# Grouped convolution in 32-row TensorE tiles on unshuffled x, with staggered tiles, in a fused convolution and mixing kernel

## What is computed

```python
# x: (64, 128, 2048) f32; c = cond_128: (64, 128); weight: (128, 32, 9); 4 groups
y = x + conv1d(x, weight, padding=4, groups=4) + (c @ c_weight.T)[:, :, None] + bias[None, :, None]

h = gelu(c @ W0 + b0); h = gelu(h @ W1 + b1)
att = softmax(h @ W2 + b2)                     # (64, 8)
agg_w = einsum('bk,koi->boi', att, weight_k)   # one 128x128 matrix per sample
agg_b = att @ bias_k
out = y + einsum('boi,bih->boh', agg_w, y) + agg_b[:, :, None]
```

## Time and profile before

| | us |
|---|---|
| profiled execution, device time | 839.29 |
| its span, first to last instruction | 837.4 |
| mean granted clock of TensorE | 0.977 of full |
| TensorE matmul busy | 766.2 (92%) |
| TensorE weight load busy | 600.9 (72%) |
| ScalarE busy | 637.2 (76%) |
| GpSimd busy | 552.1 (66%) |
| VectorE busy | 410.1 (49%) |
| DMA share of 16 engines, whole span | 91.5% |
| moved by DMA | 242.9 MB |

### The profile page before, as it was taken

How to read it: one execution, slowest core, us unless ns; L and a number is a source line. 1 busy time by engine, 2 the same in 40 slices (tenths; PEclk the granted TensorE clock), 3 DMA queues, 4 the chain that set the end, 5 groups by cost and what they waited for, 6 DMA issues and landing times.

```text
span 837.4 us, 15303 instructions
## 1 busy us (share of the span) xinstructions
PE 766.2 (92%) x5424; PEld 600.9 (72%) x5424; DVE 410.1 (49%) x299; ACT 637.2 (76%) x291; POOL 552.1 (66%) x596
## 2 busy tenths in 40 slices
PE   2659998999999999999999999999999999999994
PEld 2547776777777777777777777777777777777773
DVE  6662455445445555444555445445554444554430
ACT  7766886888778877878786787888777868866554
POOL 3289686667778767767876666668667566866620
PEclk9988999999999999999999999999999999999997
DMA  5778999999999999999999999999999999987643
GB/s 194 206 230 263 309 317 292 305 326 306 325 314 330 313 313 308 318 301 306 329 318 306 297 312 312 319 331 332 305 314 300 284 305 327 319 257 247 220 164 126
DMA packets 91011, 242.90 MB, mean 290 GB/s; under 512 B 15914, under 2 KB 58482, under 8 KB 74610
## 3 DMA queue, kind: packets, MB, share of 16 engines
q1 hardware_dynamic: 90994, 242.67, 91.5%
HBM read 101.57 MB, written 75.50 MB: 211 GB/s over the span
## 4 chain that ended last, share of the span: by engine, by line
SPq 46%; PE 20%; DMA 20%; ACT 6%; issue 6%; POOL 1%; DVE 0%; POOLq 0%
SPq L240 34%; DMA mix_dram<-mix_parts 16%; PE ps L366 12%; SPq L264 9%; PE ps L383 8%; DMA mix_rep<-mix_dram 3%; ACT z_out L448 3%; SPq L272 2%; ACT x_ph L429 1%; ACT x_cv L452 1%; DMA x_in<-in_x_dram 1%; ACT z_out L452 0%; SPq L214 0%; PE ps L353 0%; POOL mix_prod L646 0%
## 5 line engine op out<-in xcount | busy, mean ns | idle before, releaser
L448 ACT ACTIVATE z_out<-ps,par 128x2048 f32<-128x2048 f32 x64 | 253.3, 3957 | 143.0 <-PE ps L383 143.0
L515 DVE TENSOR_TENSOR y_lo<-ps,y_hi 128x1024 fp32r<-128x1024 f32 x128 | 156.4, 1222 | 305.9 <-ACT y_hi L438 305.9
L429 ACT ACTIVATE x_ph<-x_in 128x2048 f32<-128x2048 f32 x63 | 246.5, 3914 | 0.0
L366 PE MATMUL ps<-x_hi,cw_hi 128*128 128x512 f32 x768 | 228.6, 406 | 0.3 <-DVE y_lo L515 0.3
L366 PE MATMUL ps<-x_hi,cw_lo 128*128 128x512 f32 x768 | 221.3, 397 | 0.0
L366 PE MATMUL ps<-x_lo,cw_hi 128*128 128x512 f32 x768 | 220.2, 395 | 0.0
L383 PE MATMUL ps<-y_hi,mix_rep 32*128 32x512 f32 x2048 | 179.7, 418 | 41.2 <-DMA mix_rep<-mix_dram 32.8
L366 PEld LDWEIGHTS ps<-x_hi,cw_hi 128*128 128x128 f32 x768 | 141.1, 191 | 52.2 <-issue 15.0
L366 PEld LDWEIGHTS ps<-x_hi,cw_lo 128*128 128x128 f32 x768 | 145.9, 190 | 33.9
L366 PEld LDWEIGHTS ps<-x_lo,cw_hi 128*128 128x128 f32 x768 | 145.4, 189 | 33.7
L438 ACT ACTIVATE y_hi<-ps 128x1024 fp32r<-128x1024 f32 x128 | 131.0, 1023 | 47.3 <-PE ps L366 47.3
(11 more groups left out here) (69 smaller groups left out, 87.8 us busy)
## 6 DMA issues: line engine op xcount, KB each, us to landing
x_in<-in_x_dram SPq DMA_DIRECT2D x64, 1024.0 KB, 6.2
out_dram<-z_out SPq DMA_DIRECT2D x64, 1024.0 KB, 5.9
x_cv<-x_ph SPq DMA_DIRECT2D x496, 128.0 KB, 3.8
mix_rep<-mix_dram SPq DMA_DIRECT2D x256, 128.0 KB, 4.0
mix_dram<-mix_parts SPq DMA_DIRECT2D x64, 128.0 KB, 2.7
mixw_nat<-in_L_cond_weight_dram SPq DMA_DIRECT2D x1, 512.0 KB
x_cv<-x_ph SPq DMA_DIRECT2D x8, 64.0 KB, 4.2
z_out<-in_L_cond_weight_dram SPq DMA_DIRECT2D x1, 144.0 KB, 2.2
```

The source lines that it names most:

```text
L366: mm = pe.matmul(y_ps[:, g, :], w[:, g, b, :], xx[buf(s)][:, g, b:b + N], start=n == 0, stop=n == len(terms) - 1)
L429: nc.scalar.activation(x_ph[pair_buf(s)][:, :, buf(s), :], x_in[buf(s)][:, :].rearrange("c (n q) -> c q n", q=PH), ACT.Copy).then_inc(x_sp ...
L448: nc.scalar.activation(z_out[buf(s)][:, :].rearrange("c (n q) -> c q n", q=PH), z_ps[:, :, :], ACT.Identity, bias=par[s[1]][:, NK:NK + 1]) ...
L515: nc.vector.tensor_tensor(y_lo[buf(s)][:, y_halves[h], :], y_ps[:, y_halves[h], :], y_hi[buf(s)][:, y_halves[h], :].bitcast(F32), ALU.subt ...
```

## The change

The convolution takes x as it lies: partitions are channels, so one group is 32 rows of the array. For group g, output channels and the four output phases fill the 128 columns, and 12 offsets m = 0..11 (9 taps + 3 phases) are summed: `x_at` takes phase m % 4, shifted by m // 4. That makes 12 offsets x 3 terms = 36 steps of four 32-row matmuls, one of each group, in four banks. The weights for the offsets are built from `wt_hi` and `wt_lo` by copying them four times, shifted by one offset and 32 columns each, into cleared tiles; the residual x is added to the centre tap by a further matmul with the identity. `x_cv` and all its DMAs are gone.

Row tile t runs `LAG * t` = 4t steps behind tile 0, in conv and mix alike (`step`). Semaphores count y by bank and z by bank; `round_y` and `rest_y` take one bank at a time, `take_z` two. SP's slot has another order and loads four samples ahead. In the setup, conv of sample 0 starts without the conditioning network, whose matmuls stand between its steps (`between`); weights are loaded ahead of x of sample 1; the table is finished before VectorE's first slot.

```diff
-AHEAD = 7
-ACT_PHASES = 1
+AHEAD = 4
+LAG = 4
...
+    M = K + PH - 1
+    CONV, MIX = 3 * M, 3 * G
+    STEPS = CONV + MIX
...
-        x_cv = two(sb, "x_cv", [P, G, 2, N])
+        def x_at(tile, rows, m):
+            return tile[rows, m % PH, m // PH:m // PH + N]
...
             def slot(s):
-                store(after(s, -2))
-                if not is_sample(s, 0):
-                    if s[1] % 2:
-                        move_x(after(s, 3), (0, 2))
-                    else:
-                        move_x(after(s, 2), (1, 3))
-                store_mix(s)
                 load(after(s, AHEAD))
+                store_mix(s)
+                store(after(s, -2))
                 load_mix(s)
...
+            between = {4: (turn_cond,), 10: (first_layer, turn_mixw), 20: (second_layer,), 28: (third_layer,),
+                       32: (context_mixed,), 44: (attention,)}
+            def conv_step(s, g, i):
+                if not exists(s):
+                    return
+                rows = slice(Q * g, Q * g + Q)
+                if i == 0:
+                    if g == 0:
+                        pe.wait_ge(x_lo_made, done(s))
+                    at_least(pe, y_lo_made, done(s, G, lag=-2) + g + 1)
+                m, term = i // 3, i % 3
+                w, xx = ((cw_hi, x_hi), (cw_lo, x_hi), (cw_hi, x_lo))[term]
+                mm = pe.matmul(y_ps[:, g, :], w[rows, m, :], x_at(xx[buf(s)], rows, m),
+                               start=i == 0, stop=i == CONV - 1)
+                if i == CONV - 1:
+                    mm.then_inc(y_ready, 1)
+            def mix_step(s, r, i):
+                if not exists(s):
+                    return
+                rows = slice(Q * r, Q * r + Q)
+                if i == 0:
+                    if r == 0:
+                        pe.wait_ge(y_lo_made, done(s, G))
+                        pe.wait_ge(mix_loaded[buf(s)], DMA * G * (uses(s) + 1))
+                    at_least(pe, z_read, done(s, 2, lag=-2) + r // 2 + 1)
+                g, term = i // 3, i % 3
+                h, yy = ((0, y_hi), (1, y_hi), (0, y_lo))[term]
+                mm = pe.matmul(z_ps[:, r, :], mix_rep[buf(s)][rows, g, h, :], yy[buf(s)][rows, g, :],
+                               start=i == 0, stop=i == MIX - 1)
+                if i == MIX - 1:
+                    mm.then_inc(z_ready, 1)
...
             def slot(s):
-                conv(s)
-                mix(after(s, -1))
+                for i in range(STEPS):
+                    if is_sample(s, 0) and i in between:
+                        for part in between[i]:
+                            part()
+                    for t in range(PH):
+                        if i >= LAG * t:
+                            step(s, t, i - LAG * t)
+                        else:
+                            step(after(s, -1), t, i - LAG * t + STEPS)
...
+            def round_y(s, g):
+                act.wait_ge(y_ready, done(s, G, lag=-1) + g + 1)
+                if g == 0:
+                    at_least(act, z_ready, done(s, PH, lag=-2))
+                nc.scalar.activation(y_hi[buf(s)][:, g, :], y_ps[:, g, :], ACT.Copy).then_inc(y_hi_made, 1)
+            def take_z(s, h):
+                act.wait_ge(z_ready, done(s, PH, lag=-1) + 2 * h + 2)
+                pair = slice(2 * h, 2 * h + 2)
+                nc.scalar.activation(z_out[buf(s)][:, :].rearrange("c (n q) -> c q n", q=PH)[:, pair, :], z_ps[:, pair, :],
                                      ACT.Identity, bias=par[s[1]][:, NK:NK + 1]).then_inc(z_read, 1)
...
             def slot(s):
-                take_z(after(s, -2))
-                round_y(s, 0)
-                if is_sample(s, 1):
-                    split_phases((1, 1))
-                elif not is_sample(s, 0):
-                    split_phases(after(s, AHEAD - 2))
-                round_y(s, 1)
+                take_z(after(s, -2), 0)
+                take_z(after(s, -2), 1)
+                split_phases(after(s, 2))
+                for g in range(G):
+                    round_y(s, g)
...
+            for r in range(PH):
+                copy(cw_hi[:, r:r + K, Q * r:Q * r + Q], wt_hi[:, :, :].bitcast(F32)).then_inc(cw_hi_placed, 1)
```

More of the change, by code:

```diff
@@ L83, in cond_resid_kernel, with x_inner, x_halo @@
         x_in = two(sb, "x_in", [P, T])
-        x_ph = two(sb, "x_ph", [P, PH, 2, N])
-        x_cv = two(sb, "x_cv", [P, G, 2, N])
-        x_hi = two(sb, "x_hi", [P, G, N + 2], F32R)
-        x_lo = two(sb, "x_lo", [P, G, N + 2], F32R)
+        x_ph = two(sb, "x_ph", [P, PH, N])
+        x_hi = two(sb, "x_hi", [P, PH, N + 2], F32R)
+        x_lo = two(sb, "x_lo", [P, PH, N + 2], F32R)
+        def x_inner(tile):
+            return tile[:, :, 1:N + 1]
+        def x_halo(tile):
+            return tile[:, :, 0:N + 2:N + 1]
+        def x_at(tile, rows, m):
+            return tile[rows, m % PH, m // PH:m // PH + N]
         y_hi = two(sb, "y_hi", [P, G, N], F32R)
@@ L219, in load @@
                     return
-                b, split = ahead(number(s), done(s, lag=-2))
-                at_least(sp, x_split_ph, split)
+                b, taken = ahead(number(s), done(s, lag=-2))
+                at_least(sp, x_split_ph, taken)
                 sp.dma_start(x_in[buf(s)][:, :], x[b, :, :]).then_inc(x_loaded[buf(s)], DMA)
[L225 to L241, removed]
             def store_mix(s):
@@ L258, in load_mix @@
                 b = buf(s)
-                stored, mixed = ahead(DMA * (uses(s) + 1), done(s, lag=-2))
+                stored, mixed = ahead(DMA * (uses(s) + 1), done(s, PH, lag=-2))
                 sp.wait_ge(mix_stored[b], stored)
@@ L269, in store @@
                     return
-                b, read = ahead(number(s), done(s))
+                b, read = ahead(number(s), done(s, 2))
                 sp.wait_ge(z_read, read)
@@ L290, in _ @@
                 sp.dma_start(to, of).then_inc(weights_loaded, DMA)
-            sp.wait_ge(x0_by_dve, 1)
-            sp.wait_ge(x0_by_pool, PH)
+            load((0, 1))
             load((0, 2))
             load((0, 3))
[L297 to L302, removed]
             def slot(s):
+                load(after(s, AHEAD))
+                store_mix(s)
                 store(after(s, -2))
-                if not is_sample(s, 0):
-                    if s[1] % 2:
-                        move_x(after(s, 3), (0, 2))
-                    else:
-                        move_x(after(s, 2), (1, 3))
-                store_mix(s)
-                load(after(s, AHEAD))
                 load_mix(s)
@@ L332, in _ @@
[L332 to L344, removed]
+                mm = pe.matmul(ps[:, k // 4, k % 4 * P:k % 4 * P + P],
+                               cw_rep[:, k, :, :].rearrange("o q c -> o (q c)"), ident[:, :],
+                               start=True, stop=k != K // 2)
@@ new lines, in _, with turn_cond @@
+                if k == K // 2:
+                    mm = pe.matmul(ps[:, k // 4, k % 4 * P:k % 4 * P + P], ident[:, :], ident[:, :],
+                                   start=False, stop=True)
+            mm.then_inc(taps_turned, 1)
+            def turn_cond():
+                pe.wait_ge(weights_loaded, DMA * 11)
+                pe.transpose(ps[:, 4, 0:NS], cond_nat[:, :], ident[0:NS, 0:NS])
+                pe.transpose(ps[:, 4, 3 * P:3 * P + NK], mixb_sb[:, :], ident[0:NK, 0:NK])
+                pe.transpose(ps[:, 4, P:2 * P], ctxw_nat[:, :], ident[:, :]).then_inc(cond_turned, 1)
@@ new lines, in first_layer, with turn_mixw @@
+            def first_layer():
+                pe.wait_ge(cond_copied, 3)
+                pe.matmul(ps[:, 5, 0:NS], w0_sb[:, :], cond_t[:, :], start=True, stop=True).then_inc(mlp_mm, 1)
+                pe.matmul(ps[:, 4, 0:NS], ctxw_t[:, :], cond_t[:, :], start=True, stop=True).then_inc(ctx_mm, 1)
+            def turn_mixw():
+                for k in range(NK):
+                    mm = pe.transpose(ps[:, 6 + k // 4, k % 4 * P:k % 4 * P + P], mixw_nat[:, k, :], ident[:, :])
+                mm.then_inc(mixw_turned, 1)
@@ new lines, in second_layer, with third_layer @@
+            def second_layer():
+                pe.wait_ge(mlp_act, 1)
+                pe.matmul(ps[:, 5, 0:NS], w1_sb[:, :], h1[:, :], start=True, stop=True).then_inc(mlp_mm, 1)
+            def third_layer():
+                pe.wait_ge(mlp_act, 2)
+                pe.wait_ge(consts_made, 1)
+                pe.matmul(ps[0:NS, 5, 0:NK], h2[:, :], w2_sb[:, :], start=True, stop=False)
+                pe.matmul(ps[0:NS, 5, 0:NK], ones[0:1, 0:NS], b2_sb[:, :], start=False, stop=True).then_inc(mlp_mm, 1)
@@ L346, in attention, with context_mixed @@
+            def context_mixed():
+                pe.wait_ge(mixw_copied, 1)
+                pe.wait_ge(ctx_made, 1)
+                for k in range(NK):
+                    mm = pe.matmul(ps[:, 6, k * NS:(k + 1) * NS], mixw_t[:, k, :], ctx_c[:, :], start=True, stop=True)
+                mm.then_inc(ctx_mix_mm, 1)
             def attention():
```

(18 more changed lines are left out.)

258 lines of the change are left out of this document (97 added, 161 removed).

## The result

The changed kernel took 810.16 us, the median of 4 runs (808.3 to 811.2), against 839.76 for the kernel before on the same chip; the ratio is 0.9654 with a 95% interval of 0.962 to 0.9687. So it is 3.5% faster, where 776 us and 8% were forecast, and outside the range of 763 to 805. The direction was right, the size not: of 64 us there came 30. Times from here on are medians of executions in the fast state; a single one, of e3, was slow and is left out.

A forecast was written before the change was run, and what follows sets the result against it. The DMA queue, 99.5% busy, was taken to set the 12.17 us period. First mix 57.0, clock fall 1.7, 62 x 11.2 = 694.4 and tail 20.7 made 773.8; plus 1.9 and 0.8, 776 us, range 763 to 805.

The forecast's parts named there:

- Part 1: DMA queue: without the shuffle of x, 2.75 MB a sample takes 8.8 us, under TensorE's time.
- Part 2: TensorE matmuls: a step stays 0.232 us, tiling changes worth 0.42 us go, floor of the period 11.12 us.
- rival B: TensorE: the four tiles no longer run side by side, middle 0.31 us a step, 1005 us; chance 0.06.
- Part 3: TensorE's instruction issue: 384 instructions a sample and waits take 8.5 us, hidden below 11.12.
- rival C: Code fetch: TensorE's longer loop body does not fit and is fetched again, 790 to 815 us; chance 0.06.
- Part 4: ScalarE: z in two calls, y in four, split as before; 10.4 us a sample, 93% of the period.
- rival D: ScalarE bounds if halves of z cost 2.4 instead of 2.06 us: 788 to 801 us; chance 0.06.
- Part 6: SP's queue order: matrix round trip 8.4 to 10.5 us, taken as 9.5, spare 0.8; period 11.2 us.
- Rival A: The mix matrix's round trip becomes the bound, L + 11.9 = 2 periods; 807 us at L = 11.5; chance 0.15.
- L: Time from the end of the phase split through load, store_mix and load_mix to mix_rep's landing; taken as 9.5 us.
- Part 7: Setup: conv starts near 17.6 us, table done at 43.3, first mix at 57, from 53 to 60.
- Part 8: Tail from last z to last store: 20.7 us as now, from 18 to 23.

The follow-up runs named there:

- e3: Changed kernel with the mix matrix's store and its reads both issued ahead of the load and the store of z: 825.41 us, ratio 0.9786.
- e6: Kernel before without the shuffle DMAs of x, matmuls unchanged, so the output is not the reference's: 798.88 us, ratio 0.9477.
- e7: Changed kernel with the store of z moved ahead of the load, the mix matrix still behind the load: 771.59 us, ratio 0.9144.
- e9: The order of e8 with LAG 0, so the four tiles run without stagger: 804.16 us, ratio 0.9522.
- e2: Changed kernel with the store of z moved last, behind the reads of the mix matrix: 771.56 us, ratio 0.913.
- e8: Changed kernel with the store of z, then the mix matrix's store, both moved ahead of the load: 772.9 us, ratio 0.9155.

## Why the prediction was wrong

- *What bounds the kernel before*: right that it is the shuffle's DMAs; e6 shows it, 12.15 to 11.51 us a period without them. That it is their bytes, by the 99.5%, is not shown against their issues on SP's queue.
- *Part 1, DMA falls under TensorE's time*: right, 74.4% busy for the three quarters that 8.8 / 11.78 gives. But a queue that isn't full isn't free: at 74.4% a load took 6.2 us beside a store, in e7 5.0 without it.
- *Part 2, the step and the tiling changes*: right. e7's period of 11.13 and e6's of 11.51 differ by 0.38 us, 0.42 were forecast, and TensorE is never idle in either. Steps whose tiles read different tensors cost what the mix steps did, so **rival B is out**, and with it the 3.07x of the Trainium skill (TensorE: Matmul & The Clock Gate, Part 3, measured speedup) for this kernel: at 0.302 us a step the period would be 14.5, measured is 11.1 where nothing waits.
- *Part 3, issue, and rival C*: 384 instructions and the waits fit into 11.1 us, and no instruction packet came between 160 and 700 us, so rival C is out.
- *Part 4, ScalarE*: z halves 2.12 us for 2.06, banks of y 0.60 for 0.59, split 3.87. Its sum of 10.5 never was the bound, so rival D is out; the stagger's part in it is shown by e9.
- *Part 6* is **the step that failed**. It gave the matrix's round trip 8.4 to 10.5 us (its terms add up to 8.5 to 10.5), "I take 9.5", and had 0.8 us spare. Measured are 11.4, 1.1 over what the period allows, and 11.55 on average. The mis-sized term is mix_dram's landing, priced from a row of a transfer behind one store with nothing beside it: 4.1 to 4.6, measured 6.1. The load's issue took 0.7 for 0.5, and the reads 4.6 for 3.9 and the 0 to 1.5 of the store, which was seen as a delay of the reads only. In the changed order load and store are issued 1.2 us apart, run together, and the load, behind which the matrix stands, lands after 6.2 us instead of about 5; e2 and e7 part the two, mix_dram lands after 4.9, and the period is TensorE's.
- *Rival A* had the mechanism and the formula, and at L = 11.5 gave 11.7 and 807 us; it came to 11.4, 11.78 and 810. So the mechanism was in the text, with a chance of 0.15, and the range ended at 805. A spare of 0.8 us beside bounds 2.1 us wide was no ground for allowing only 0.08 us a period.
- *Part 7, setup*: 58.27 for 57, within 53 to 60; conv starts at 17.2 (17.6), and the table's last piece ends at 43.1 (43.3). *Part 8*: 18.0, the end of the range that I had for staggered steps at full clock.

What stays open: whether bytes or issues bounded the kernel before; how LAG 2 moves L from 11.55 to 11.66; and how the engines divide themselves between a load and a store, of which only the sums were measured.

## What to carry to other kernels

When a change frees the bound (here the moves of x), look for the loop of latencies that is next, add its worst terms, and price each transfer by rows in which the same neighbours are in flight, not by the quietest one at hand, and by the mean of many samples, not by one. What cost time here wasn't a small transfer behind a large one: in e7 the matrix still stands 0.6 us behind the load, and TensorE decides. It was two large ones in flight together with it. Moving a megabyte store away from the other was worth 0.051 in the ratio, about 43 us, more than the whole change gave. Look also at a queue that waits for its own transfer: in e3 that wait alone closed a cycle of 11.9 us. Change one part at a time: the tiling and the DMAs were one edit, and only e6 and e7 tell that without the moves a period is 0.6 us shorter, and with the new tiling another 0.4.

## What the runs showed that I had not expected

- A 128 KB write issued 0.5 us behind two 1 MB transfers took 8.7 us to land (e3), behind one of them 4.9 (e7), in the quiet setup 1.7 (its shortest). In e3 and e7 it landed 0.35 and 0.36 us behind the megabyte just ahead of it in the queue.
- The stagger of the tiles could cost time. It lengthens the z end of the round trip loop by 4 steps while it takes away the wait for y_lo, so its worth depends on which of the two decides. In the changed kernel they come out nearly even, 11.78 against 11.69 us a period, and a first mix 3.9 us later adds to the loss; where the order of the DMAs is good, it won 31 us (e8 against e9).
- Taking the shuffle's moves out of the kernel before and leaving its matmuls alone gave more (5.2%) than the whole change (3.5%).
